# A decoder layer on one core: queries by way of DRAM, a second taps buffer, a new order of SyncE's list, and the key-query copy moved to ScalarE

## What is computed

```
mixed = silu(causal_conv1d(x @ w_qkv, conv_w))      # 4 taps per channel
q, k, v = split(mixed)                              # 16 key heads, 32 value heads, 128 wide
q, k = l2norm(q), l2norm(k)
g = -exp(A_log) * softplus(a + dt_bias); beta = sigmoid(b)
for t in tokens:                                    # done in chunks of 128 tokens
    St = St * exp(g_t)
    St = St + k_t (v_t - k_t St) * beta_t
    o_t = q_t St
core = o * rsqrt(mean(o * o) + eps) * norm_weight * silu(x @ w_z)
x = x + core @ w_out
```

## Time and profile before

| | us |
|---|---|
| median of 3 runs | 3450.14 |
| lowest and highest | 3445.16, 3451.03 |
| the profiled execution | 3444.88 |
| its span, first to last instruction | 3443.1 |
| PE busy in the span | 3236.4 (94%) |
| DVE, POOL, ACT busy | 2300.1, 1920.2, 1666.4 |

### The profile page before, as it was taken

How to read it: one execution, slowest core, us unless ns; L and a number is a source line. 1 busy time by engine, 2 the same in 40 slices (tenths; PEclk the granted TensorE clock), 3 DMA queues, 4 the chain that set the end, 5 groups by cost and what they waited for, 6 DMA issues and landing times. The chain is left out here.

```text
span 3443.1 us, 59910 instructions
## 1 busy us (share of the span) xinstructions
PE 3236.4 (94%) x20064; PEld 2115.5 (61%) x20064; DVE 2300.1 (67%) x3494; ACT 1666.4 (48%) x5111; POOL 1920.2 (56%) x1888
## 2 busy tenths in 40 slices
PE   5899999999999999998999999999988999999999
PEld 2567666676667666676667666676763444454444
DVE  6788788887888788787878787787870000024453
ACT  2456566565656566565656565565662000011232
POOL 2677677777777677776767677776760000001032
PEclk8999999999999999999999999999999999999999
DMA  2233333333333333333333333333334222211001
GB/s 98 57 79 94 88 83 84 88 88 87 81 82 91 90 82 85 84 86 93 78 83 84 83 96 84 84 77 98 82 96 173 98 106 89 98 37 61 1 13 37
DMA packets 469200, 282.30 MB, mean 82 GB/s; under 512 B 311808, under 2 KB 410240, under 8 KB 463360
## 3 DMA queue, kind: packets, MB, share of 16 engines
q1 hardware_dynamic: 467600, 271.39, 29.6%
q10 hardware_dynamic: 1296, 7.09, 0.5%
HBM read 173.17 MB, written 88.34 MB: 76 GB/s over the span
## 5 line engine op out<-in xcount | busy, mean ns | idle before, releaser
L762 PE MATMUL acc<-xT,wc 128*128 128x512 f32 x2048 | 944.0, 605 | 9.2 <-DVE d_kks L1092 7.2
L1019 DVE SCALAR_TENSOR_TENSOR d_conv<-acc,wc,d_conv 128x511 f32<-128x511 f32 (+2 forms) x768 | 566.1, 737 | 94.0 <-ACT d_conv L1198 82.4
L762 PEld LDWEIGHTS acc<-xT,wc 128*128 128x128 f32 x2048 | 375.0, 193 | 384.3 <-issue 383.7
L775 PE MATMUL acc<-wc,xT 128*128 128x256 f32 x2048 | 473.4, 385 | 0.0
L1058 DVE STREAM_TRANSPOSE d_em<-d_dm 128x1024 f16<-128x1024 f16 x256 | 314.6, 1229 | 196.0 <-ACT d_dm L1249 195.9
L775 PEld LDWEIGHTS acc<-wc,xT 128*128 128x128 f32 x2048 | 379.8, 190 | 45.6
L1249 ACT ACTIVATE d_dm<-acc 128x512 f16<-128x512 f32 x384 | 227.2, 592 | 233.4 <-PE acc L820 233.3
L1546 PE MATMUL acc<-t_area 128*128 128x512 f32 x768 | 332.5, 593 | 2.2 <-ACT t_area L1995 2.2
L1065 DVE CAST_PREDICATED d_zm<-cons,d_tz 128x512 f16<-128x512 int32 x384 | 264.1, 688 | 90.6 <-PE d_tz L807 84.0
L1198 ACT ACTIVATE d_conv<-acc,wc 128x512 f32<-128x512 f32 x256 | 175.1, 684 | 300.0 <-PE acc L762 176.3
L2052 POOL TENSOR_SCALAR t_veps<-t_mv 128x1 f32<-128x1 f32 x32 | 9.7, 303 | 546.8 <-DVE t_mv L1791 546.8
(11 more groups left out here) (226 smaller groups left out, 6951.1 us busy)
## 6 DMA issues: line engine op xcount, KB each, us to landing
d_decay<-decay_rows SPq DMA_DIRECT2D x64, 512.0 KB, 5.1
v_rows<-d_vb SPq DMA_DIRECT2D x256, 128.0 KB, 2.8
d_vn<-v_rows SPq DMA_DIRECT2D x64, 512.0 KB, 3.7
core_rows<-d_ob SPq DMA_DIRECT2D x1024, 32.0 KB, 1.7
t_area<-core_rows SPq DMA_DIRECT2D x30, 1024.0 KB, 4.8
wc<-in_w SPq DMA_DIRECT2D x96, 256.0 KB, 3.0
k_rows<-d_kf SPq DMA_DIRECT2D x256, 64.0 KB, 3.9
d_kn<-k_rows SPq DMA_DIRECT2D x64, 256.0 KB, 2.9
```

The lines of the kernel that those rows point to most:

```text
L762: last = nc.tensor.matmul(bank(TILE[j])[:, :], wtile(j, k), xT[:, k, r % B * S:(r % B + 1) * S], start=k == 0, stop=k == KT - 1)
L775: last = nc.tensor.matmul(bank(f"z{j}")[:, i * GV * P:(i + 1) * GV * P].rearrange("p (h n) -> p h n", h=GV), xT[:, k, r % B * S + (2 * j + ...
L1019: nc.vector.scalar_tensor_tensor(c[:, d:S], bank(TILE[j])[:, 0:S - d], tap(j, KS - 1 - d), c[:, d:S], ALU.mult, ALU.add).then_inc(taps, 1)
```

## The change

1. `move_q` is replaced by `store_q(s)`, four DMAs from qf into a DRAM tensor q_rows, and `load_q(s)`, one DMA back into qn.
2. The taps have a tile of their own, taps2, with two halves used by turns. SP's wait before it loads them is now for the taps of four units earlier.
3. SP's slot has another order: `store_q(s)`, `store_o` of unit n - 4, `load_q(s)`, then the weights of tiles 1 and 0 and the taps, the decay rows, `store_k`, `load_k`, `next_weights(n, 3)`, and the rest as before without `store_o` at its end. One more slot is added behind the last.
4. ACT's `first_output(s)` stands ahead of the eight `o_scale` pieces and of `k_square`.
5. `copy_kq` leaves DVE (one instruction of 128x512) and goes to ACT as four pieces of 128x128, behind `k_square(n)` and ahead of `copy_d(m, 2)`.
6. The element-wise results of `o_square`, which nobody reads, go into the bytes of qf in place of junk and ob. So `o_square(f, ...)` waits until `store_q` of the next unit has landed, `flip_q` waits for the squares of two units before, and `flip_o` and `o_square` lose a wait.

The core of the diff:

```
             def slot(n, project, invert, recur, finish):
+                if recur:
+                    store_q(back(n, 2))
+                if finish:
+                    store_o(back(n, 4))
+                if recur:
+                    load_q(back(n, 2))
                 if invert:
                     next_weights(back(n, 1), 1)
                 if project:
                     next_weights(n, 0)
                 if invert:
                     next_weights(back(n, 1), TILES)
-                if recur:
-                    move_q(back(n, 2))
-                if project:
-                    next_weights(n, 3)
...
                     load_k(n)
+                    next_weights(n, 3)
...
-                if finish:
-                    store_o(back(n, 3))
                 if project:
                     next_weights(n, 2)
...
-                        sp.wait_ge(taps, at(n, 12, 12))
+                        wait(sp, taps, at(back(n, B), 12, 12))
...
+            def store_q(m):
                 sp.wait_ge(v_flipped, at(m, 2, 2))
+                wait(sp, q_moved, at(back(m, 1), MOVED, MOVED))
+                for a in range(NC):
+                    sp.dma_start(q_dram[m[1] % 2].rearrange("b i a n -> a i b n")[a],
+                                 qf[a * 32:(a + 1) * 32].rearrange("p b c j -> p b (c j)")).then_inc(q_moved, 16)
+
+            def load_q(m):
+                sp.wait_ge(q_moved, at(m, MOVED, SENT))
                 wait(sp, q_squares, at(back(m, 1), NC, NC))
-                for a in range(NC):
-                    for b in range(NC):
-                        sp.dma_start(qn[b * 32:(b + 1) * 32, a].rearrange("p c j -> p (c j)"),
-                                     qf[a * 32:(a + 1) * 32, b].rearrange("p c j -> p (c j)")).then_inc(q_moved, 16)
+                sp.dma_start(qn[:, :, :, :].rearrange("p a c j -> p (a c j)"),
+                             q_dram[m[1] % 2].rearrange("b i a n -> (b i) (a n)")).then_inc(q_moved, 16)
...
+            def copy_kq(m):
+                act.wait_ge(kq_done, count(m))
+                wait(act, p_ready, at(back(m, 1), GV, GV))
+                for c in range(NC):
+                    nc.scalar.activation(chunk(kqs, c), chunk(bank("kq"), c), ACT.Copy, scale=rk[m[1] % 2][:, 0, c:c + 1]).then_inc(kqs_ready, 1)
...
-                if (c, h) in ((1, 0), (0, 1)):
-                    out = junk[:, h, :]
-                else:
-                    wait(act, stored, at(back(s, 1), STORES, STORES))
-                    out = ob[:, c, h * NC:(h + 1) * NC, :].rearrange("p b j -> p (b j)")
+                if s[0] * ROUND + s[1] < ITERS - 1:
+                    act.wait_ge(q_moved, at(back(s, -1), MOVED, SENT))
+                out = squared[:, h * NC + c, :]
...
                 if invert:
                     copy_d(m, 1)
+                if recur:
+                    first_output(s)
                 if finish:
                     o_scale(f, 0)
                     o_scale(f, 1)
                 if project:
                     k_square(n)
-                if recur:
-                    first_output(s)
+                if invert:
+                    copy_kq(m)
                 if invert:
                     copy_d(m, 2)
```

More of the change, by code:

```diff
@@ L30 @@
 GCOLS = WCOLS + 4 * KS
+TAPS = 4 * KS
 LEVELS = 6
@@ L39 @@
 STORES = 16 * NC * NC
-MOVED = 16 * NC * NC
+MOVED = 16 * (NC + 1)
+SENT = 16 * NC
 C_ID, C_LE, C_GT, C_ONE, C_LT, C_LEV = 0, P, 2 * P, 3 * P, 4 * P, 5 * P
@@ L111, in bc, with head @@
     return ap.unsqueeze(axis).to_broadcast(shape)
-def head(nc, a, xT, tabs, cons, nw, wc, w_loaded, taps_loaded):
+def head(nc, a, xT, tabs, cons, nw, wc, taps2, w_loaded, taps_loaded):
     with ExitStack() as ctx:
@@ L152, in _ @@
                 cols = slice(j * KT * P, (j + 1) * KT * P) if j < TILES else slice(WCOLS, GCOLS)
-                sp.dma_start(wc[:, cols], a["w"][0, :, cols]).then_inc(w_loaded[j] if j < TILES else taps_loaded, 16)
+                dst = wc[:, cols] if j < TILES else taps2[:, 0, :]
+                sp.dma_start(dst, a["w"][0, :, cols]).then_inc(w_loaded[j] if j < TILES else taps_loaded, 16)
             sp.wait_ge(rows_ready, B)
@@ L317, in _, with delta_rule @@
                 nc.scalar.activation(spread(Q_CDEC, b), gathered(pss[2], b), ACT.Exp).then_inc(act_chain, 1)
-def delta_rule(nc, xT, tabs, cons, nw, wc, w_loaded, taps_loaded, acc, early_loaded, early_weighed, decay_dram, w_dram, k_dram, v_dram, core_dram, wout):
+def delta_rule(nc, xT, tabs, cons, nw, wc, taps2, w_loaded, taps_loaded, acc, early_loaded, early_weighed, decay_dram, w_dram, k_dram, q_dram, v_dram, core_dram, wout):
     with ExitStack() as ctx:
@@ L343, in delta_rule @@
         oo = many("oo", 2, [P, GV, NC, P])
-        junk, kqs, kks = sb("junk", [P, GV, P], BF16), sb("kqs", [P, S]), sb("kks", [P, S])
+        kqs, kks = sb("kqs", [P, S]), sb("kks", [P, S])
         kss, qss, rkt, rk = sb("kss", [P, NC]), sb("qss", [P, NC]), sb("rkt", [P, NC]), many("rk", 2, [P, 2, NC])
         qf, qn = sb("qf", [P, NC, NC, 32]), sb("qn", [P, NC, NC, 32])
+        squared = qf[:, :, :, :].rearrange("p b c j -> p (b c j)").bitcast(BF16).rearrange("p (n d) -> p n d", d=P)
         eq = many("eq", 4, [P, NC])
@@ L394, in wtile, with tap @@
             return wc[:, (j * KT + k) * P:(j * KT + k + 1) * P]
-        def tap(j, k):
-            return wc[:, WCOLS + j * KS + k:WCOLS + j * KS + k + 1]
+        def tap(n, j, k):
+            return taps2[:, (n[0] * (ROUND // B) + n[1] // B) % 2, j * KS + k:j * KS + k + 1]
         def tab(n, q, h=None, c=None):
@@ L441, in delta_rule @@
                       "z0": (z_silued, "z_silued", 0), "z1": (z_silued, "z_silued", 1),
-                      "kk": (kk_copied, "once", 0), "kq": (kqs_ready, "once", 0)}
+                      "kk": (kk_copied, "once", 0), "kq": (kqs_ready, "squares", NC - 1)}
         CONV_ORDER = ("k", "v1", "v0", "q")
@@ L480, in load_weights @@
                 src = w_dram[g, :, cols] if isinstance(g, int) else w_dram[bass.ds(g, 1), :, cols].rearrange("a p n -> (a p) n")
-                sp.dma_start(wc[:, cols], src).then_inc(w_loaded[j] if j < TILES else taps_loaded, 16)
+                dst = wc[:, cols] if j < TILES else taps2[:, g % 2, :]
+                sp.dma_start(dst, src).then_inc(w_loaded[j] if j < TILES else taps_loaded, 16)
             def load_decay(n):
@@ L588, in _ @@
             for u in range(ITERS):
-                slot((u // ROUND, u % ROUND), True, u >= 1, u >= 2, u >= 3)
+                slot((u // ROUND, u % ROUND), True, u >= 1, u >= 2, u >= 4)
             slot((ROUNDS, 0), False, True, True, True)
@@ L592, in _ @@
             slot((ROUNDS, 2), False, False, False, True)
+            slot((ROUNDS, 3), False, False, False, True)
             sp.wait_ge(stored, STORES * ITERS)
@@ L612, in k_norm @@
                 pool.wait_ge(rk_ready, at(n, 3, 1))
-                wait(pool, kqs_ready, count(n, 2))
+                wait(pool, kqs_ready, at(back(n, 2), NC, NC))
                 wait(pool, v_scaled, at(back(n, 2), NC, NC))
@@ L661, in p_full @@
             def p_full(m, h):
-                pool.wait_ge(kqs_ready, count(m))
+                pool.wait_ge(kqs_ready, at(m, NC, NC))
                 pool.wait_ge(gamc_ready, nth(m, "gamc_ready", h))
@@ L1018, in convolve @@
                     dve.wait_ge(taps, nth(n, "taps", 3 * j + d - 2))
-                nc.vector.scalar_tensor_tensor(c[:, d:S], bank(TILE[j])[:, 0:S - d], tap(j, KS - 1 - d),
+                nc.vector.scalar_tensor_tensor(c[:, d:S], bank(TILE[j])[:, 0:S - d], tap(n, j, KS - 1 - d),
                                                c[:, d:S], ALU.mult, ALU.add).then_inc(taps, 1)
@@ L1037, in flip_q @@
                 dve.wait_ge(silued, nth(m, "silued", 1))
-                wait(dve, q_moved, at(back(m, 1), MOVED, MOVED))
+                wait(dve, o_squares, at(back(m, 2), GV * NC, GV * NC))
+                wait(dve, q_moved, at(back(m, 1), MOVED, SENT))
                 nc.vector.transpose(qf[:, :, :, :], qT[third(m)][:, :].rearrange("p (c b j) -> p b c j", c=NC, b=NC)).then_inc(v_flipped, 1)
@@ L1092, in copy_kk @@
                 nc.vector.tensor_tensor(by_chunk(kks), by_chunk(bank("kk")), per_token(rk[n[1] % 2][:, 0, :]), ALU.mult).then_inc(kk_copied, 1)
[L1094 to L1098, removed]
             def output(s, c):
@@ L1159, in slot @@
                     level_z(m, 2)
-                    copy_kq(m)
                 if recur:
@@ L1197, in first_tap @@
                 free(act, n, TILE[j], CONV_ORDER, CONV_BUFFER, SILUED, CONV_LAG)
-                nc.scalar.activation(conv_of(TILE[j])[:, :], bank(TILE[j])[:, :], ACT.Copy, scale=tap(j, KS - 1)).then_inc(tap0, 1)
+                nc.scalar.activation(conv_of(TILE[j])[:, :], bank(TILE[j])[:, :], ACT.Copy, scale=tap(n, j, KS - 1)).then_inc(tap0, 1)
             def silu(n, j):
@@ L2091, in decoder_layer @@
         with ExitStack() as ctx:
```

(7 more changed lines are left out.)

2 lines of the change are left out of this document (removed).

## The result

The kernel after takes 3465.4 us (median of 4 runs, 3464.1 to 3469.0), the kernel before on the same chip 3450.6 (4 runs, 3445.2 to 3455.5). The ratio is 1.0045, with a 95% interval of 1.0028 to 1.0062: slower by 0.45%. The forecast was 3476 in 3453 to 3530, with slower at 0.80. The profiled execution took 3466.2 us with a span of 3464.4, against 3443.1 before.

A forecast was written before the change was run, and what follows sets the result against it. PE was taken to bound the kernel, at 36.33 us a slot with 153.3 us of loss above that. Terms +74 - 57 + 9 + 0 = +26 us on 3444.9, plus 5.3 to the median, gave 3476, range 3453 to 3530.

The forecast's parts named there:

- The group starts: First slot of each group: taps issued 4.6 us later in SP's list, PE's attend waits longer; +74 us over 15.
- The term's second part, the clock: At each group's first slot, PE's granted clock may lose a little more than now: 0.3 us taken each.
- The rule weighed there: Clock penalty is throttled time times lost clock share; at the groups' first slots it would give 94 us, not 74.
- The second kind of wait: In 33 other slots read_q(s, 1) waits for first_output, behind k_square waiting for keys; its end wins 57 us.
- the prediction's second reason: Keys come back sooner, since the 16 move_q issues (10.02 us) no longer stand between the weights and store_k.
- The key-query copy: Four pieces on ACT ahead of copy_d(m, 2) slip it 0 to 0.2 us; +9 us, bounds 0 and 26.
- The squares: ACT's o_square(f, 1, 0) must wait until the q stores land; 0 us taken, range 0 to +39.
- the squares' wait shows: Rival, chance 0.13: q stores land as late as key stores, ACT's squares wait; +39 us more, 3515.
- the whole cover of 1.02 us: ACT's room for late squares: 0.63 us idle before copy_d(s, 5), plus 0.39 between its end and refine.
- there is nothing to see: Rival, chance 0.07: the taps slip 3 to 3.5 us in place of 4.6, time within 7 us of before.
- the taps' stall disappears: Rival, chance 0.04: the second buffer makes the taps early, nearly all 153 us go; 3306.
- the queue does not set the group's wait: Rival, chance 0.08: taps land as soon after flip_q as now, leaving -57 + 9 = -48 us; 3402.

The follow-up runs named there:

- experiment 1: The kernel after with the taps' load moved to the head of SP's slot, ahead of store_q: 3294.3 us, ratio to before 0.9533.
- experiment 2: The kernel after with the taps issued behind 8 of the 16 output stores: 3372.6 us.
- experiment 3: The kernel before with only first_output moved ahead of o_scale and k_square: 3442.5 us, ratio 0.9961.
- experiment 4: The kernel after with first_output moved back behind k_square: 3462.5 us.
- Experiment 5: The kernel after with the taps at the head of SP's slot, and copy_kq back on DVE as one instruction: 3293.3 us, ratio to before 0.9544.
- experiment 10: The kernel after with the taps at the head of SP's slot, and 12 of the 16 output stores ahead of the query stores: 3462.5 us.
- experiment 9: The kernel after with the taps at the head of SP's slot, and 8 of the 16 output stores ahead of the query stores: 3320.3 us.

## Why the prediction was right, and where its sizes were off

**The group starts (+74 forecast, +75.6 measured).** The mechanism is shown by experiments 1 and 2: with the taps out of the chain the wait is gone, and with half of the stores in front it is 2.7 us in place of 8.6. The slip in the slot that I read is 4.97 us for the 4.6 worked out from the keys' issues; SP's pauses of 0.5 us in the new chain, for the 0.05 taken, make the difference. On average PE's `attend` waits 4.44 us longer (128.3 - 61.7, over 15). The term's second part, the clock, was small in the forecast and is somewhat larger: of 5.04 us per group start 4.44 are this wait and 0.60 the rest (clock, refill and smaller waits together), for the 0.3 taken. The slot in the windows has a granted clock of 0.89, where rows of before had 0.92 and 0.96: more of it ran at 1.2 GHz. The two errors, 0.16 too much and 0.3 too little a group start, partly cancel.

The rule weighed there, that the loss grows with the throttled time (the Trainium skill, TensorE: Matmul & The Clock Gate, Terms), would have had 94 for this term. Its direction agrees with the trace: the mean clock of the 15 group starts fell from 0.94 to 0.89. Its size does not, since the term came out at 75.6. The windows of PE's wait in the slot shown, and of the 7 us behind it, say why:

```profile
1460.54:1469.02 8.48, 0.00 (x1) 0.03 (x1) 1.21 (x3) 1.93 (x8) 0.00 (x0) 0.76 0.41 94
1469.02:1476.00 6.98, 6.98 (x27) 4.50 (x28) 6.20 (x10) 4.62 (x13) 4.98 (x5) 0.56 0.35 90
```

The clock falls to 1.2 GHz while PE still waits (0.50 from 1466 to 1468). At 0.76 some 4 us of the wait are slow, in which PE had nothing to do, and at 0.56 some 6 us of work behind it. Over the 15 group starts I estimate from such windows that the slow time behind the wait went from 3.9 to 5.6 us, and that inside it from 0.9 to 4.7. Most of the longer slow time thus fell into the wait, where it costs nothing.

**The second kind of wait (-57 forecast, -56.7 measured).** The 45 slots stood 1.26 us above 36.33 and now stand 0.02 above. The prediction gave both edits as its cause. Experiments 3 and 4 divide it: `first_output` alone moves the wait to `level_z` and leaves 37.32, and without it the kernel after keeps its 36.34. What did it is that the keys come earlier, as the prediction's second reason had it, and by the issue times mostly because those of `move_q` are gone.

**The key-query copy (+9 forecast, about 0 measured).** This is the term that was mis-sized. Its range went down to 0, and 0 is what it is: 0.02 x 45 = 0.9 us is all that the slots which start no group have above 36.33, and 0.7 of it stands in the two slots in which the squares wait longest. The four pieces took 1.11 us, within the 1.0 to 1.2 of the estimate, and `copy_d(m, 2)` starts at the same 26.65 us after `flip_q` as before (1358.76 - 1332.11 in the earlier trace rows). The step that failed is "the slip is 0 to 0.2 us", of which I took 0.15: a sum of rounded rows can't tell 0.1 us, and the range's lower end was the right one. Experiment 5 gives the copy's price as nothing.

**The squares (0 forecast, under 1 us measured).** ACT's first square waits for the query stores 1.22 and 1.34 us in two slots, which last 36.61 and 36.73: 0.7 us above 36.33 together. The prediction names a wait on q_rows of over 1 us as a sign of being wrong. These two slots and the sum of 3.6 us meet it, so the stores are not always in time; in the other 58 slots the wait is 0.56 us or less and nothing is lost. The query stores took 1.8 us to land, near the 32 KB output stores' 1.7 and not the keys' 3.9 of before. The DMA issues of the kernel after (KB each, median us to landing):

```profile
core_rows<-d_ob SPq DMA_DIRECT2D x1024, 32.0 KB, 1.7
...
k_rows<-d_kf SPq DMA_DIRECT2D x256, 64.0 KB, 3.5
...
q_rows<-d_qf SPq DMA_DIRECT2D x256, 64.0 KB, 1.8
```

The same 64 KB takes 1.8 us in one place and 3.5 in another. The decay load of 512 KB stands right in front of the keys and not in front of the queries, and the distance to it varies in the traces. In the kernel after the key stores start within 1.3 us of the start of the decay load's issue in 44 slots and land in 3.9 us on average; in the 15 group starts, where they start 3.8 us behind it, they land in 1.8. In experiment 10 they start 4.4 us or more behind it in every slot, and the median is this:

```profile
k_rows<-d_kf SPq DMA_DIRECT2D x256, 64.0 KB, 1.8
```

So the time to landing goes with the decay load still being under way, as the prediction assumed. What the two transfers share, the traces don't say.

**The sum.** The forecast was 10.6 us too high. The terms gave +26 for a span that grew by 21.3, which is 4.7 of it. Another 5.3 is the distance of the profiled execution of before from its median, which I added; the execution profiled after lies 0.8 above its own median, which is the rest but for rounding. One execution does not say on which side of the median the next one lies.

**The rivals.** That the queue does not set the group's wait is refuted by experiments 1 and 2. That the squares' wait shows needs stores that land 2.9 us or more after their issue. That is where `copy_d(s, 5)` begins to be late; with the whole cover of 1.02 us PE begins to lose at 3.3, so the rival's condition was set too low. The median was 1.8, and experiments 9 and 10 show what late stores cost. That there is nothing to see is refuted by the 14.8 us between the medians and the slip of 4.97. That the taps' stall disappears was the rival with the smallest chance, at 3306. The prediction says that it needs another place in SP's list than the diff gives, and experiment 1 puts it there, at 3294.

## What to carry to other kernels

A DMA that an engine waits for must be placed by what stands in front of it in the issuing engine's list, and each issue has a price: in the chain here 0.39 to 0.49 us, and 11.3 us from the start of the first query store's issue to the end of the taps'. A second buffer for its target showed no worth while its load stayed behind those issues, and some 52 us ahead of them; look for the stretch in which the issuing engine idles, and put the load there. The same price works the other way: five issues in place of 16 ahead of the key stores brought the keys 5.6 us forward. When a wait is to be removed by a shift in one engine's list, look at what else stands behind the same late data, since the wait moves to it. And a new piece of work in an engine that waits for the bound engine costs nothing up to the length of that wait, which the brackets of the timeline give directly. Hold it against the longest wait of a slot and not the average: experiment 9 had an average at the edge of the cover and still lost 17 us.

## What the runs showed of the hardware

- The 16 issues of 32 KB stores took SP 7.88 us (median of 60 slots), 0.49 each, in the kernel after as in experiment 1. Single slots reach 9.47 and 9.77, so the 7.77 and 8.31 of the two slots shown are no difference of the kernels. The 16 pieces of `move_q`, 16 KB each and from tile to tile, took 10.24, 0.64 each.
- With 8.5 us without work in it, the slot of 48 us has a granted clock of 0.89, and the fall comes while PE still waits. With 15 such stretches removed the clock is 1.00 over 2180 us.
- From the end of the issue of the same 8 KB load to `first_tap` it took 1.3 us behind 32 KB stores, 1.3 with nothing in front for 14 us, and 2.3 behind two transfers of 256 KB. The landing of a store of 64 KB took 3.9 us within 1.3 us of a load of 512 KB and 1.8 when 3.8 us or more behind it.
